# A transformer layer with experts: batches kept once in fp32 from the norm to attention, gate scores with the gate's weights stationary

## The reference

```python
x = L0_attn_x                                  # (32, 512, 256), float32
xn = layernorm(x)
# attention: q, k, v = xn @ W + b, 16 heads of 16; relative positions
score = ((q + u) @ k.T + relative_shift((q + v) @ pos.T)) / sqrt(16)
att = (softmax(score) @ val) @ Wo + bo
# experts: scores = xn @ gate_w (8 experts), probs = softmax(scores)
g, m = top_k(probs.transpose(0, 2, 1), 128)    # each expert takes 128 of a batch's 512 tokens here
h = gelu(xn[m] @ w1) @ w2                      # hidden size 1024
ffn = scatter_add(g * h)                       # rounded to bfloat16
return x + att + ffn
```

## Time and profile before

| | |
|---|---|
| median of 3 runs | 5658.87 us (5654.17 to 5681.21) |
| the profiled execution | 5688.57 us, its span 5686.9 us |
| busy: PE, DVE, ACT, POOL | 92%, 65%, 61%, 24% of the span |
| mean granted clock of TensorE | 0.95 of full speed |
| DRAM traffic | 708.72 MB read, 674.50 MB written |
| norm phase | 0 to 231.8 us |
| route phase | to 308.6 us |
| attention | to about 3760 us |

### The profile page before, as it was taken

The page is one execution under the profiler, slowest core; times in us unless marked ns, Lnnn a source line. Parts: engine busy times, 40 slices in busy tenths (PEclk is TensorE's granted clock), DMA queues, the critical chain, the costliest instruction groups (busy, mean ns, idle before and its releaser), DMA issues. The chain is left out here.

```text
span 5686.9 us, 129597 instructions
## 1 busy us (share of the span) xinstructions
PE 5212.5 (92%) x43044; PEld 3952.8 (70%) x43044; DVE 3668.2 (65%) x8040; ACT 3461.5 (61%) x5147; POOL 1348.1 (24%) x1000
## 2 busy tenths in 40 slices
PE   8669999999999999999999999979999999999855
PEld 8636666666666666666666666658888988888744
DVE  6748878878778778778778878854333333333233
ACT  1138878878778778778778778844444443444211
POOL 1011111111111111111111111114444444444355
PEclk9979989999999999999999999989999999999987
DMA  8749999999999999999999999943232233322398
GB/s 293 300 172 360 343 319 338 327 343 339 323 340 335 323 330 339 325 332 342 322 334 339 333 343 335 351 148 68 56 58 53 47 59 57 54 48 44 64 298 260
DMA packets 321255, 1392.49 MB, mean 245 GB/s; under 512 B 41760, under 2 KB 136608, under 8 KB 180000
## 3 DMA queue, kind: packets, MB, share of 16 engines
q1 hardware_dynamic: 262176, 1282.68, 65.9%
q0 software_dynamic: 53760, 83.92, 8.2%
q10 hardware_dynamic: 4608, 16.78, 0.8%
HBM read 708.72 MB, written 674.50 MB: 243 GB/s over the span
## 5 line engine op out<-in xcount | busy, mean ns | idle before, releaser
L801 DVE CUSTOM_DVE_ANT_0 att_shifted<-att_sp,att_shifted 128x512 f32<-128x512 f32 x2048 | 1333.3, 685 | 296.0 <-PE att_sp L956 215.4
L687 ACT ACTIVATE att_shifted<-att_shifted,att_mn 128x512 f32<-128x512 f32 x2048 | 1359.3, 717 | 86.0 <-issue 85.7
L682 ACT ACTIVATE att_xo<-att_xp 128x1024 f32<-128x1024 f32 x1024 | 1048.4, 1024 | 547.5 <-PE att_xp L944 546.9
L811 DVE COPY att_pt<-att_tp 128x512 f32<-128x512 f32 x1536 | 1014.3, 687 | 263.9 <-PE att_tp L977 263.0
L977 PE MATMUL att_tp<-att_ident,att_shifted 128*128 128x128 f32 x8192 | 1155.1, 285 | 1.0 <-ACT att_shifted L687 0.4
L977 PEld LDWEIGHTS att_tp<-att_ident,att_shifted 128*128 128x128 f32 x8192 | 905.9, 144 | 306.8 <-issue 293.4
L1238 DVE TENSOR_TENSOR ffn_hp<-ffn_hf,ffn_hp 128x512 fp32r<-128x512 f32 x512 | 355.0, 693 | 924.6 <-ACT ffn_hf L1205 924.5
L956 PE MATMUL att_sp<-att_kd,att_qu 64*128 64x512 f32 x2048 | 778.0, 458 | 102.3 <-issue 77.1
L1203 ACT ACTIVATE ffn_hp<-ffn_up 128x512 fp32r<-128x512 f32 x512 | 305.9, 597 | 925.7 <-PE ffn_up L1296 917.7
L944 PE MATMUL att_xp<-att_pos,att_qv 64*128 64x512 f32 x2048 | 858.2, 458 | 9.0 <-ACT att_xo L682 8.9
L1270 PE MATMUL ffn_yp<-ffn_w2p,ffn_hp 128*128 128x256 f32 x6144 | 830.4, 285 | 28.1 <-DVE ffn_w2p L1246 22.8
(11 more groups left out here) (111 smaller groups left out, 5234.1 us busy)
## 6 DMA issues: line engine op xcount, KB each, us to landing
xs_d<-att_xo SPq DMA_DIRECT2D x512, 1026.0 KB, 10.3
att_shifted<-xs_d SPq DMA_DIRECT2D x512, 1024.0 KB, 8.7
xt_d<-norm_xts SPq DMA_DIRECT2D x32, 1024.0 KB, 4.0
att_xt<-xt_d SPq DMA_DIRECT2D x32, 1024.0 KB, 10.4
norm_xin<-in_L_attn_x_dram POOLq DMA_DIRECT2D x32, 512.0 KB, 6.0
xn_d<-norm_xn SPq DMA_DIRECT2D x32, 512.0 KB, 4.2
ffn_d<-route_zero SPq DMA_DIRECT2D x8, 2048.0 KB, 21.1
att_d<-att_osb SPq DMA_DIRECT2D x512, 32.0 KB
```

Source lines behind the costliest of these rows:

```text
L682: act.activation(xo[:, kk % NW, 2 * half:2 * half + 2, 1:S + 1], xp[:, :, :], ACT.Copy).then_inc(x_out, 1)
L687: act.activation(shifted[:, kk % NX, t], shifted[:, kk % NX, t], ACT.Exp, bias=mn[:, kk % NX, t:t + 1], scale=-1.0).then_inc(exp_done, 1)
L801: dve.tensor_tensor_reduce(out=shifted[:, kk % NX, t], in0=sp_[:, t % 2], in1=shifted[:, kk % NX, t], scale=-0.25, scalar=-NEG, op0=ALU.ad ...
L811: dve.tensor_copy(pt[:, t], tp[:, t % 2]).then_inc(t_out_dve, 1)
```

## The change

The norm phase no longer splits the turned batch. ACT copies it once in fp32; SP stores it once, 512 KB, and `xt_d` in DRAM has half its size. The scores are made in fp32, with the gate weights stationary and the 512 tokens of a batch moving: two matmuls a batch, one for each half of the features. The weights are 8 columns inside a block of 32 whose other columns are zero; for the batch with number v in its group of four the window into the padded block is moved by 8 v, so that four batches accumulate into 32 rows of PSUM, and 32 batches fill two banks. At the end ACT copies both banks once into `scores_t`, which holds experts in rows and tokens in columns. All buffers have four slots for two, loads of x run four batches ahead, the statistics of batch b+1 are taken ahead of the normalization of batch b, the store of a turned batch is issued behind that of the next normalized one, and PE's program is written out for all batches.

The route phase first turns the scores back, tokens in rows, by eight transposes into PSUM (`gate`); DVE reads them there.

In attention SP loads the batch once (512 KB) into `xf`, and POOL makes the high and the low part, at the start for batches 0 and 1 and then after the u queries of the first and of the third tile of each iteration. SP's wait for projections ahead of the load is gone; it waits for the split of the batch before. POOL waits for the projections, and PE for `xt_low`.

```diff
 norm phase, NS = 4 slots, PACK = 32
-        gws = m.sb("gws", [P, 2, DC, NE], F32R)
-        xts = m.sb("xts", [P, 2, 2, DC, S], F32R)
+        gw = m.sb("gw", [P, DC, 2 * PACK - NE])
+        xts = m.sb("xts", [P, NS, DC, S])
 SP
+                sp.wait_ge(padded, 1)
+                sp.dma_start(gw[:, :, PACK - NE:PACK], gate_w.rearrange("(c p) e -> p c e", p=P)).then_inc(const_in, 16)
+                def store_xt(b, s):
+                    wait_alone(sp, copied, b + 1)
+                    sp.dma_start(xt_d[bass.ds(b, 1)].rearrange("o p c t -> p (o c) t"), xts[:, s]).then_inc(xt_stored[s], 16)
                         wait_alone(sp, normed, b + 1)
                         sp.dma_start(xn_d[...], xn[:, s]).then_inc(xn_stored[s], 16)
-                        wait_alone(sp, low, b + 1)
-                        sp.dma_start(xt_d[...], xts[:, s].bitcast(F32)).then_inc(stored[s], 16)
+                            store_xt(b - 1, (s - 1) % NS)
 POOL
-                        wait_alone(pool, normed, b - 1)
+                        wait_alone(pool, normed, b - NS + 1)
 DVE
-                def low_part(b, s):
-                    dve.wait_ge(high, b + 1)
-                    dve.tensor_tensor(xts[:, s, 1], tp[:, s], xts[:, s, 0].bitcast(F32), ALU.subtract).then_inc(low, 1)
+                        if s < NS - 1:
+                            statistics(i, b + 1, s + 1)
+                        elif not (isinstance(i, int) and i == B // NS - 1):
+                            statistics(i + 1, b + 1, 0)
                         dve.wait_ge(root, b + 1)
                         dve.reciprocal(rstd[:, s], sd[:, s]).then_inc(recip, 1)
 ACT
+                def copy_turned(i, b, s):
+                    act.wait_ge(turned, b + 1)
+                    wait(act, xt_stored[s], i * 16)
+                    wait(act, scored, b - NS + 1)
+                    act.activation(xts[:, s], tp[:, s % 2], ACT.Copy).then_inc(copied, 1)
+                act.wait_ge(scored, B)
+                act.activation(scores_t[:, :, :], gp[:, :, :], ACT.Copy).then_inc(kept, 1)
 PE
-                def scores(b, s):
-                    pe.wait_ge(low, b + 1)
-                    wait(pe, kept, b - 1)
-                    for t in range(TT):
-                        for k, (w, a) in enumerate(SPLITS):
-                            for c in range(DC):
-                                ins = pe.matmul(gp[:, s, t * NE:(t + 1) * NE], xts[:, s, a, c, t * P:(t + 1) * P],
-                                                gws[:, w, c, :], start=(k == 0 and c == 0), stop=(k == 2 and c == DC - 1))
+                def scores(b):
+                    pe.wait_ge(copied, b + 1)
+                    group, v = b // 4, b % 4
+                    rows = slice(group % 4 * PACK, (group % 4 + 1) * PACK)
+                    for c in range(DC):
+                        ins = pe.matmul(gp[rows, group // 4, :], gw[:, c, PACK - NE - v * NE:2 * PACK - NE - v * NE],
+                                        xts[:, b % NS, c, :], start=(v == 0 and c == 0), stop=(v == 3 and c == DC - 1))
                     ins.then_inc(scored, 1)
 route phase, PE ahead of everything, DVE waits for by_token
+                for h in range(2):
+                    for t in range(TT):
+                        ins = pe.transpose(gate[:, h, t], scores_t[:, h, t * P:(t + 1) * P], ident[:, :])
+                ins.then_inc(by_token, 1)
 attention phase, SP
-                    sp.dma_start(xt[:, s].bitcast(F32), xt_d[...]).then_inc(xt_in[s], 16)
+                    wait_alone(sp, xt_low, b)
+                    sp.dma_start(xf[:, :, :], xt_d[bass.ds(b, 1)].rearrange("o p c t -> p (o c) t")).then_inc(xt_in, 16)
                         if kk % H == 4 and not last:
-                            wait_alone(sp, k_full, i * TILES + (kk // H + 1) * (H // MH))
-                            wait_alone(sp, v_full, (i * 2 + kk // H + 1) * 2)
-                            load_xt(i * 2 + 2 + kk // H, kk // H)
+                            load_xt(i * 2 + 2 + kk // H)
 attention phase, POOL
+                def split_xt(b, s):
+                    wait_alone(pool, xt_in, (b + 1) * 16)
+                    wait_alone(pool, q_full, (b - 1) * (H // MH))
+                    wait_alone(pool, k_full, (b - 1) * (H // MH))
+                    wait_alone(pool, v_full, (b - 1) * 2)
+                    pool.tensor_copy(xt[:, s, 0], xf[:, :, :]).then_inc(xt_high, 1)
+                    wait_alone(pool, xt_high, b + 1)
+                    pool.tensor_tensor(xt[:, s, 1], xf[:, :, :], xt[:, s, 0].bitcast(F32), ALU.subtract).then_inc(xt_low, 1)
+                split_xt(0, 0)
+                split_xt(1, 1)
                             keys(i, t)
                             with_u(i, t)
+                        if t % 2 and not last:
+                            split_xt(i * 2 + 2 + t // 2, t // 2)
                         if not (last and t + 1 >= TILES):
                             with_v(i, t + 1)
 attention phase, PE
-                    pe.wait_ge(xt_in[t // DC % 2], (i + t // TILES + 1) * 16)
+                    pe.wait_ge(xt_low, i * 2 + t // DC + 1)
```

More of the change, by code:

```diff
@@ L104, in shape_constants, with norm_phase @@
     return sinusoid, ident, first_row, spread
-def norm_phase(nc, x, gate_w, ident_d, xn_d, xt_d, gate):
+def norm_phase(nc, x, gate_w, ident_d, xn_d, xt_d, scores_t):
+    NS = 4
+    PACK = P // 4
     with ExitStack() as ctx:
@@ L124, in norm_phase @@
         const_in = m.sem("const_in")
-        split = m.sem("split")
-        x_in = [m.sem(f"x_in{s}") for s in range(2)]
+        padded = m.sem("padded")
+        eps_set = m.sem("eps_set")
+        x_in = [m.sem(f"x_in{s}") for s in range(NS)]
         stat = m.sem("stat")
@@ L182, in body @@
-                def body(i):
-                    for s in range(2):
-                        b = i * 2 + s
-                        dve.wait_ge(x_in[s], (i + 1) * 16)
-                        for t in range(TT):
[L188 to L191, removed]
-                        if not (isinstance(i, int) and b == 0):
-                            low_part(b - 1, 1 - s)
+                dve.memset(gw[:, :, :], 0.0).then_inc(padded, 1)
@@ L249, in body @@
-                def body(i):
-                    for s in range(2):
-                        b = i * 2 + s
-                        pe.wait_ge(normed, b + 1)
-                        wait(pe, low, b - 1)
-                        for c in range(DC):
-                            for t in range(TT):
-                                ins = pe.transpose(tp[:, s, c, t * P:(t + 1) * P], xn[:, s, t, c * P:(c + 1) * P], ident[:, :])
-                        ins.then_inc(turned, 1)
-                        if not (isinstance(i, int) and b == 0):
-                            scores(b - 1, 1 - s)
@@ new lines, in _ @@
+                for b in range(B):
+                    s = b % NS
+                    pe.wait_ge(normed, b + 1)
+                    wait(pe, copied, b - 1)
+                    for c in range(DC):
+                        for t in range(TT):
+                            ins = pe.transpose(tp[:, s % 2, c, t * P:(t + 1) * P], xn[:, s, t, c * P:(c + 1) * P], ident[:, :])
+                    ins.then_inc(turned, 1)
+                    if b:
+                        scores(b - 1)
+                scores(B - 1)
@@ L286, in route_phase @@
         tb = m.ps("tb", [P, 2, 2, P])
+        gate = m.ps("gate", [P, 2, TT, P])
         const_in = m.sem("const_in")
@@ L450, in attention_phase @@
         edge_set = m.sem("edge_set")
-        xt_in = [m.sem(f"xt_in{s}") for s in range(2)]
+        xt_in = m.sem("xt_in")
+        xt_high = m.sem("xt_high")
+        xt_low = m.sem("xt_low")
         q_full = m.sem("q_full")
```

130 lines of the change are left out of this document (62 added, 68 removed).

## The result

The changed kernel takes 5576.52 us (median of 4 runs, 5571.18 to 5588.76) where the kernel before took 5663.61 beside it: a ratio of 0.9846, 95% interval 0.9816 to 0.9876. That is 87 us less, where 64 were forecast (5595; range 5552 to 5638).

The account below looks back on a forecast made before the run. PE, read as at the lower clock level, bounds the norm phase, with DMA second; full PE paces attention between loop ends. Median 5,658.9 - 61 (norm) + 4 (route) - 7 (attention) gives 5,595 us; range 5,552 to 5,638.

Parts of the forecast that it names:

- Norm phase: Norm phase: 32 batches of 5.24 us plus 3 us end at 171 us instead of 231.8, 61 us gained.
- the bound given for it (148): Norm phase: best case, 4.54 us a batch x 32 + 3 = 148 us, 84 us gained.
- DMA, "4.54 to 4.81 us, at a share of 0.96 4.9": Norm phase: DMA time a batch after dropping 512 KB of 2,048 KB; 4.9 us with loads four batches ahead.
- Clock, "0.6 x 4.9 + 0.4 x 5.75": Norm phase: PE at the lower clock level 40% of the time, as in the last phase; 5.24 us a batch.
- Route phase: Route phase start: identity load, eight transposes and two hand-overs add 3.9 us; reading PSUM costs nothing.
- POOL's split: Attention: POOL's cast and subtraction take 3.9 us a batch, 126 us in all, but cost nothing, with 7.4 us to spare.
- rival (c): Attention: the split comes late for v and stops PE, 32 times 10 us, 5,915 us; chance 0.03.
- (d): Attention: POOL's split stretches DVE's work, 32 x 3.8 = 121 us, 5,716 us; chance 0.02.
- Attention: Attention: 16.8 MB of loads less give at least 0, at most 20 us; 7 us gained was taken.
- Rival (e): Attention gives back half or more of the gain as transfers fall differently at loop ends; 5,635 to 5,655 us; chance 0.08.
- (a): Norm phase: PE stays at the lower clock level, the phase ends at 197, about 5,625 us; chance 0.15.
- (b): Attention: DMA backlog also lengthens loop ends, so 3 us return in each of 15 iterations, 45 us; 5,557; chance 0.09.

Follow-up runs that it names:

- second store: The changed kernel, but each turned batch is stored a second time to a place nobody reads; 5594.65 us, ratio 0.9869 to the kernel before.
- attention's part alone: The kernel before with its old norm and route phases, plus one fp32 copy stored once and the changed attention; 5645.95 us, ratio 0.9976.
- fp32, same side: Old norm order, two slots, activations still stationary, but fp32 scores in 8 matmuls a batch for 24; changed attention; 5622.47 us, ratio 0.9805 to before.
- two slots: The changed kernel with two slots for four in the norm phase, nothing else; 5767.24 us, ratio 1.0165 to the kernel before.
- same side, written out: The kernel "fp32, same side" with PE's norm program written out for all 32 batches instead of a loop; 5654.14 us, ratio 0.9897 to before.
- changed, five comparisons: The changed kernel measured five times against the kernel before, twice with empty PE instructions that the profiles do not show; ratios 0.9836 to 0.9853.
- second load: The changed kernel, but attention loads every batch twice, the second copy unused; 5647.14 us, ratio 0.9855 to the kernel before.

## Why the prediction was right, and which terms were mis-sized

**Norm phase: right in kind, mis-sized.** Forecast 171 us and -61; measured 141.3 and -90.5, beyond the bound given for it (148). The bound did move from PE to the DMA engines, as the second store shows. A batch of 3.97 us is outside the 4.5 to 5.75 us that the prediction named as a sign of being wrong. Two terms of the sum were off:

- *DMA, "4.54 to 4.81 us, at a share of 0.96 4.9".* Measured 3.97. It took what the DMA engines did under a PE-bound phase, 2,048 KB in 6.05 busy us (347 GB/s), as what they can do. Fed by four slots they moved 390 GB/s at a printed share of 1.04, and 387 with the old traffic. 1,536 KB at 390 GB/s are 4.0 us. The row for it was there: 409 GB/s at the route phase's start. It was used for the 512 KB that fell away and not for the 1,536 KB that stay.
- *Clock, "0.6 x 4.9 + 0.4 x 5.75".* The mix of 40% at the lower level was taken from the last phase. Measured: the clock rose at about 17 us and was 0.98 in the window. Four scoring records took 1.90 us (the forecast's figure for the upper level was 1.89). The last phase, from which the mix was taken, had 0.80. The mix cost 0.34 us a batch, 11 us; the DMA term 0.93 us a batch, 30 us. Together they are 41; the first batch and the end took 14 us (141.3 - 32 x 3.97) where 3 were put down, which leaves the 30 us missed.

In the sum, attention (6 us) and the route phase (1 us) came out on the other side, so 23 us of it are left. That the time lies inside the range, 24 us above its lower end, is in part luck: the range reached that far down by allowing attention a gain of 20 us, and it was the norm phase that went past its own bound.

**Route phase: right.** Forecast +3.9, measured +4.8; the first reduction starts 4.9 us after the phase's start. PE waits for both of its loads, `first_row` too, and starts after 3.0 us; the transposes take 1.83. Reading PSUM costs nothing (1.23 us against 1.22).

**POOL's split: right.** 1.04 + 2.38 us and a gap make 3.6 where 3.9 was forecast. POOL is idle behind each split that stands ahead of queries, once for only 0.75 us; v is never late for it, so rival (c) fell. DVE's additions last 685 ns in the median as before (678 to 693 in all 2,048), so (d) fell too.

**Attention: near in sum, its parts open.** Forecast -7; measured -1.4 in the first comparison. The four later ones of the same program give -8, -9, -14 and -5 in the same way, -7 in the mean of five (by the ratios -1 to -10, mean -6). The prediction thought of it as one small gain. It costed nowhere that PE's program is written out, though that stood in the change, and it did not read the second wait of the kernel before. The pair of fp32 kernels shows that writing out raises that wait and the time (0.4 to 1.4%). With attention's part alone, whose second wait is as before, 22 us are gained (11 to 33). A reading would be that the changed kernel has this gain too and loses it again to some 20 us more of second wait. It is argued, not shown, and the record speaks in part against it. Here is what each kernel's ratio leaves behind the norm and route phases, all of them with attention changed as in the changed kernel:

| kernel | behind norm and route, us | second wait |
|---|---|---|
| fp32, same side | -63 (-80 to -45) | 6.6 |
| second store | -34 (-48 to -20) | 41.3 |
| attention's part alone | -22 (-33 to -11) | 22.6 |
| two slots | -16 (-32 to 1) | 41.2 |
| same side, written out | -10 (-35 to 14) | 60.0 |
| changed, five comparisons | -1 to -10 | 45 to 56 |

The wait alone does not put them in order: the second store has the changed kernel's PE program and its wait, and gains more than attention's part alone. What attention's gain consists of stays open; the test of the traffic, 7 to 11 us with noise of 22, does not settle it. Rival (e), which gives back half the gain or more, did not come.

**Rivals.** (a) fell: the clock rose within the first batch's scores. What it was based on holds where the activations stay stationary: in the fp32 kernel of the old side PE is 98% busy with 8-column matmuls, and the transposes stay at 1.97 us. (b) fell: the three us an iteration did not come back, and the second load bounds what traffic can give.

**Where the gain is.** One fp32 form in place of three products gives 49 us of it (231.8 to 182.6), with the order, the two slots and the stationary side as they were; DVE's subtraction and half of the turned batch's store go with it. The other 41 come from the swapped operands, the new order and the four slots together: less PE time, a clock that rises, and DMA at its rate. No run tells apart what each is worth; with two slots the swapped kernel's norm phase is 106 us longer than the old one.

**What was not tried.** The best parts together, the changed norm phase with PE's program as a loop: 142 us of norm with a second wait near 7 would save some 40 us more by an estimate from the waits of these rows (45 less 7), if all of the wait reaches the time, which the second store puts in doubt. The 32 PSUM rows that a group of batches writes are chosen in the written-out code, and a loop would have to choose them by a register.

## What to carry to other kernels

The DMA rate seen in a phase that another engine bounds is no measure of what DMA can do there: take it from the fastest stretch of the profile, and look whether enough buffers keep the queues fed. A reordering that takes work on batch b+1 ahead of batch b must be counted in buffers first: here the same order took 141 us with four and 338 with two, where the old kernel took 232. Writing out a loop in one phase is not free for the others: compare the waits for "issue" at every later loop's end, and hold what they say against the medians.

## What the runs showed of the hardware

- **Norm phases in which PE is full stayed at the lower clock level (1.2 GHz).** Through 182 to 240 us with 8-column matmuls, PE 98 to 100% busy in the records, eight transposes took 1.97 us; in the changed kernel, PE busy for 59.66 of 80 us, they took 1.10 from the third batch on. The windows printed a granted clock of 1.00 for the full ones and 0.98 for the changed kernel: durations tell the level, the printed value at a program's start does not. The Trainium skill, "TensorE: Matmul & The Clock Gate", Part 1, lets the clock follow how busy PE has been; these phases, busy by the profile, did not rise, and the measurement decides.
- **512 KB DMAs sustained 390 GB/s** with one stream of loads and two of stores over four slots, each landing in 7.7 to 8.8 us, and 387 GB/s with one more store a batch; the share of the DMA engines is then printed as 1.04 and 1.03. With two slots the rate was 150 GB/s.
- **PE's code ahead of a loop changes a wait of 0 to 7 us at its ends**: with nothing else changed, 6.6 us in sum with 96 matmul records of norm code and 60 with 768. Kernels that differ in more than that have 20 to 27 with 128 and 41 to 56 with 384. This does not make it a rule of size; the place in the code may count as well.
